# The last attention layer in eight half-batch stages, with softmax sums from ScalarE

## The reference

```python
for e in range(4):                       # quarters of 256 tokens
    xe = x[:, e * n:(e + 1) * n, :]
    xn = _layernorm(xe, norm_w, norm_b)
    m = d // 2 ** e                      # 256, 128, 64, 32 features
    xm = xn[..., :m]
    qs.append(einsum('bnm,dm->bnd', xm, q_w[:, :m]) + q_b)   # ks, vs alike
...                                      # 8 heads of 32, scale d ** -0.5
probs = softmax(q k^T * scale);  attn_out = probs v
out_e = einsum('bnm,om->bno', attn_out[quarter e, :m], o_w[:m, :m]) + o_b[:m]
return concat(pad(out_e) + x_e)          # then _layernorm(x + that)
```

## Time and profile before

| | us |
|---|---|
| median of 3 runs | 2969.61 (2962.3 to 2972.91) |
| profiled execution | 2967.14 |
| its span | 2965.0 |
| PE busy | 2357.0 (79%) |
| DVE busy | 1519.0 (51%) |
| ACT busy | 895.3 (30%) |
| POOL busy | 600.1 (20%) |

### The profile page before, as it was taken

The page is one execution under the profiler, slowest core; times in us unless marked ns, Lnnn a source line. Parts: engine busy times, 40 slices in busy tenths (PEclk is TensorE's granted clock), DMA queues, the critical chain, the costliest instruction groups (busy, mean ns, idle before and its releaser), DMA issues. The chain is left out here.

```text
span 2965.0 us, 44749 instructions
## 1 busy us (share of the span) xinstructions
PE 2357.0 (79%) x18544; PEld 1454.3 (49%) x18544; DVE 1519.0 (51%) x2671; ACT 895.3 (30%) x1265; POOL 600.1 (20%) x340
## 2 busy tenths in 40 slices
PE   3888888999898885856567389898288888898896
PEld 1344544444444443735455245665155555555553
DVE  2445444445454543454645334655566566765662
ACT  0233332333333333423333122221032343333332
POOL 3121111112221101010101033333211122112212
PEclk7899999999999998878888799999588999999998
DMA  6455555444544534566566510110442453245230
GB/s 141 86 101 101 109 103 112 100 94 102 106 108 94 99 60 143 187 199 239 183 232 210 175 59 29 57 57 1 147 118 73 138 145 89 85 138 147 66 91 31
DMA packets 235288, 337.57 MB, mean 114 GB/s; under 512 B 14816, under 2 KB 172880, under 8 KB 234832
## 3 DMA queue, kind: packets, MB, share of 16 engines
q1 hardware_dynamic: 232272, 334.07, 42.4%
q10 hardware_dynamic: 2816, 0.65, 0.1%
HBM read 206.10 MB, written 127.93 MB: 113 GB/s over the span
## 5 line engine op out<-in xcount | busy, mean ns | idle before, releaser
L444 ACT ACTIVATE l0a_probs<-l0a_slot 128x1024 f32<-128x1024 f32 (+1 forms) x256 | 247.4, 970 | 419.5 <-PE l0a_slot L606 419.3
L1620 ACT ACTIVATE l1f_probs<-l1f_slot 128x1024 f32<-128x1024 f32 x240 | 241.0, 1022 | 428.1 <-PE l1f_slot L1793 293.3
L501 DVE TENSOR_REDUCE l0a_rowmax<-l0a_slot 128x4 f32<-128x1024 f32 (+1 forms) x256 | 293.4, 1156 | 126.6 <-PE l0a_slot L606 123.7
L1683 DVE TENSOR_REDUCE l1f_rowmax<-l1f_slot 128x1 f32<-128x1024 f32 x240 | 287.7, 1219 | 100.5 <-PE l1f_slot L1779 100.3
L601 PE MATMUL l0a_slot<-l0a_maskT,l0a_ident 128*128 128x512 bf16 (+1 forms) x512 | 161.6, 400 | 73.7 <-issue 67.9
L1793 PE MATMUL l1f_slot<-l1f_Qs,l1f_Ks 128*128 128x256 f32 x960 | 185.5, 320 | 40.8 <-DVE l1f_rowmax L1683 16.6
L1793 PEld LDWEIGHTS l1f_slot<-l1f_Qs,l1f_Ks 128*128 128x128 f32 x960 | 142.7, 202 | 110.9 <-DVE l1f_rowmax L1683 29.9
L1779 PE MATMUL l1f_slot<-l1f_Ks,l1f_Qs 96*128 96x512 f32 x480 | 172.4, 453 | 29.3 <-DMA l1f_Qs<-kq_rows 16.5
L601 PE MATMUL l0a_slot<-l0a_mask,l0a_ident 128*128 128x512 bf16 (+1 forms) x512 | 150.3, 376 | 25.7 <-issue 23.4
L404 POOL TENSOR_TENSOR l0a_turned<-l0a_turned 128x512 f32<-128x512 f32 x32 | 40.7, 1273 | 634.8 <-DVE l0a_turned L487 634.8
L1738 PE MATMUL l1f_os<-l1f_probs,l1f_V 128*32 128x256 f32 x1920 | 165.6, 397 | 2.0 <-ACT l1f_probs L1620 1.1
(11 more groups left out here) (186 smaller groups left out, 4018.7 us busy)
## 6 DMA issues: line engine op xcount, KB each, us to landing
expert_outputs<-l0f_inter SPq DMA_DIRECT2D x64, 512.0 KB, 2.6
l0f_wide<-expert_outputs SPq DMA_DIRECT2D x32, 1024.0 KB, 9.6
l0a_Qs<-qk_rows SPq DMA_DIRECT2D x96, 256.0 KB, 7.9
l0a_Ks<-qk_rows SPq DMA_DIRECT2D x96, 256.0 KB, 15.0
l1f_Ks<-kq_rows SPq DMA_DIRECT2D x48, 512.0 KB, 6.9
l0f_f<-in_dram SPq DMA_DIRECT2D x10, 2048.0 KB, 15.4
qk_rows<-l0a_hi SPq DMA_DIRECT2D x32, 512.0 KB, 2.8
qk_rows<-l0a_lo SPq DMA_DIRECT2D x32, 512.0 KB, 4.2
```

The source lines that it names most:

```text
L444: exp_ready.by(act.activation(probs[:, t % 2, HG * g:HG * g + HG, 0:reach, :], s[:, :, 0:reach, :], ACT.Exp, scale=SCALE))
L501: max_ready.by(dve.reduce_max(rowmax[:, t, :, 2 * g:2 * g + 2], s[:, :, :, first:2 * P], AX))
L1620: exp_done.by(act.activation(probs[:, half, u - FIRST[i], :], s[:, :], ACT.Exp, scale=SCALE))
L1683: max_done.by(dve.reduce_max(rowmax[:, 2 * u + t:2 * u + t + 1], s[:, :], AX))
```

## The change

In the fourth layer:

1. The hand-written list is replaced by eight equal stages, two a batch, of tr tiles of half a batch, four pv of the half before, and the nat tiles of three stages later; the class `Schedule` walks it, and offsets say which sequence a step belongs to (-1 to 2). K and Q are bounced in one stage and stacked in the next.
2. The sums of the softmax come from the nat tiles. After the maximum, ACT takes the exponential of the nat tile in place, with the negated maximum as bias, and adds along the keys. The tile's last reader is now ACT.
3. The pv step has no matmul of ones. The 8 or 6 sums of a batch are inverted by DVE as 128x8 values and spread over 32 columns a unit; PE transposes that (step `R`, two matmuls with the identity), ACT copies it to SBUF, and DVE multiplies.
4. Wq and its bias are scaled once, so the exponentials take no scale; the sign of the maxima row changes.
5. Placing the maxima (the small DMA on ACT's queue) is a step of its own, in the stage after the transpose.
6. In all layers POOL clears the layer's semaphores at its end.

```diff
+    front = {0: [(1, "xT", 0), (1, "xT", 1), (1, "xT", 2)],
+             1: [(2, "load", 0), (1, "k", 0), (1, "q", 0)],
+             2: [(1, "stack k", 0), (1, "stack q", 0), (-1, "out", 0), (-1, "out", 1)],
+             3: [(1, "k", 1), (1, "q", 1), (-1, "finish", 0)],
+             4: [(1, "stack k", 1), (1, "stack q", 1), (1, "rest of q", 0), (1, "v", 0)],
+             5: [(0, "again", 0), (1, "v", 1), (2, "statistics", 0)],
+             6: [],
+             7: [(2, "normalise", 0)]}
+    for s in range(NSTAGE):
+        i, half = divmod(s, 2)
+        n = len(BATCHES[i])
+        tr = [(0, "tr", 2 * FIRST[i] + n * half + u) for u in range(n)]
+        o, was = divmod(s - 1, NSTAGE)
+        pv = [(o, "pv", HKT * was + j) for j in range(HKT)]
+        o, part = divmod(s + 3, NSTAGE)
+        units = range(FIRST[part // 2], FIRST[part // 2] + len(BATCHES[part // 2]))[2 * (part % 2):2 * (part % 2) + 2]
+        nat = [(o, "nat", 2 * u + t) for u in units for t in range(2)]
+        row = merged(nat[:len(nat) // 2], tr[:2]) + pv[:2] + merged(nat[len(nat) // 2:], tr[2:]) + pv[2:]
+        row = merged(row, front[s])
+        if s % 2 == 0:
+            row += [(0, "R", i - 1) if s else (-1, "R", NB - 1), (o, "mT", part // 2)]
+            placing = o, part // 2
+        else:
+            row[4:4] = [(placing[0], "place", placing[1])]
+            row[6:6] = [(placing[0], "recip", placing[1])]
+        steps += row
...
+            return {"nat": (sum_done, i + 1), "tr": (exp_done, i + 1), "mT": (maxT_ready, i + 1), "out": (summed, (1, NE)[i % 2]),
...
+                if kind == "nat":
+
+                    s = schedule.slot(step)
+                    max_done.wait(act, X, i + 1)
+                    sum_done.by(act.activation(s[:, :], s[:, :], ACT.Exp, bias=negmax[:, i:i + 1].bitcast(f32),
+                                               accum_out=sums[:, i:i + 1]))
...
-                    exp_done.by(act.activation(probs[:, half, u - FIRST[i], :], s[:, :], ACT.Exp, scale=SCALE))
+                    exp_done.by(act.activation(probs[:, half, u - FIRST[b], :], s[:, :], ACT.Exp))
+                if kind == "R":
+                    rows = DH * len(BATCHES[i])
+                    spread_done.wait(act, X, i + 1)
+                    ao_ready.wait(act, X - (i < 2), (3, NB + 1, 1, 2)[i])
+                    spread_ready.by(act.copy(spread[0:rows, i % 2, :], OS[i % 2][0:rows, 1, :]))
...
-                    max_done.by(dve.reduce_max(rowmax[:, 2 * u + t:2 * u + t + 1], s[:, :], AX))
+                    s = arrived(dve, X, step)
+                    max_done.by(dve.reduce_max(negmax[:, i:i + 1], s[:, :], AX, negate=True))
...
+                if kind == "recip":
+                    units = len(BATCHES[i])
+                    cols = slice(2 * FIRST[i], 2 * FIRST[i] + 2 * units)
+                    sum_done.wait(dve, X, cols.stop)
...
-                    for what in range(2):
-                        for u in range(n):
-                            h = BATCHES[i][u][0]
-                            lhsT = ones[:, :] if what else V[:, parity, kt, DH * h:DH * h + DH]
+                    for u in range(units):
+                        h = BATCHES[b][u][0]
+                        last = mm(OS[b % 2][DH * u:DH * u + DH, 0, :], V[:, parity, kt, DH * h:DH * h + DH],
+                                  probs[:, half, u, QW * j:QW * j + QW], start=kt == 0, stop=kt == NT - 1,
```

More of the change, by code:

```diff
@@ L25, in ps, with clear @@
         return ctx.enter_context(nc.psum_tensor(f"{layer}_{name}", shape, dtype))
+    sems = []
+    def clear():
+        nums = sorted(s.num for s in sems)
+        for n in nums:
+            if n - 1 not in nums:
+                nc.gpsimd.sem_clear(range(n, next(m for m in itertools.count(n) if m not in nums)))
+    ctx.callback(clear)
     def sem(name):
-        return ctx.enter_context(nc.semaphore(f"{layer}_{name}"))
+        sems.append(ctx.enter_context(nc.semaphore(f"{layer}_{name}")))
+        return sems[-1]
     return sb, ps, sem
@@ L1336, in tr @@
[L1336 to L1366, removed]
@@ L1377, in nested_width_attention_layer @@
+    slotted = ("xT", "k", "q", "v", "nat", "mT", "tr", "out")
     with ExitStack() as ctx:
@@ L1400, in nested_width_attention_layer @@
         own_ln = LayerNorm(sb, sem, "own", setup, 1)
-        slots = [ps(f"slot{i}", [P, 1024]) for i in range(NSLOT)]
+        schedule = Schedule(steps, slotted, [ps(f"slot{i}", [P, 1024]) for i in range(3)], NSEQ)
+        arrived = schedule.arrived
         OS = [ps(f"os{i}", [P, 2, QW]) for i in range(2)]
@@ L1420, in nested_width_attention_layer @@
+        inverted = signal("inverted", NB); recip_ready = signal("recip_ready", NB); spread_done = signal("spread_done", NB)
+        spread_ready = signal("spread_ready", NB); ao_ready = signal("ao_ready", NB + 1)
         summed = signal("summed", NE)
[L1422 to L1428, removed]
@@ L1460, in loop, with reader @@
[L1460 to L1475 removed]
+        def reader(name):
+            kind, i = name
+            return {"nat": (sum_done, i + 1), "tr": (exp_done, i + 1), "mT": (maxT_ready, i + 1), "out": (summed, (1, NE)[i % 2]),
+                    "xT": (xT_ready[i % 3], None), "v": (v_ready, i + 1), "k": (lo_ready, 2 * i + 1), "q": (lo_ready, 2 * i + 2)}[kind]
@@ L1806, in piece @@
                             col += w
-                (lead_filled if is_ahead else filled).by(last)
-            loop(pe, piece)
+                schedule.put(step, last)
+            schedule.loop(pe, piece)
 def four_layers(nc, x, wq, wk, bq, bk, wv, bv, wo, bo, cos, sin, mask, maskT, ident, ident16,
```

448 lines of the change are left out of this document (204 added, 244 removed).

## The result

The kernel after takes 3077.1 us (median of 4 runs, 3071.96 to 3084.18), the kernel before 2968.02 beside it: ratio 1.0366, 95% interval 1.033 to 1.0402. Slower, as forecast, but by 109 us and not by 33, and outside the range (3053). Its profiled execution has a span of 3078.1 us.

A forecast was written before the change was run, and what follows sets the result against it. Bound: waits on the ring of three PSUM tiles, held by the natural exponential. Full-clock period 102.7 us, 107 with clock; 2251 + 7p gives 3000 us. Range 2925 to 3053 us, to hold eight tenths.

The forecast's parts named there:

- The sign: Whole kernel: slower, 3000 us, 33 over the profiled time; chances slower 0.60, same 0.14, faster 0.26.
- What is removed and added on each engine: Fourth layer, per sequence: PE loses 14.7 us and gains 1.8, to about 70; ACT comes to 69, DVE to 59.
- The pieces of the slot's life: Natural tile's PSUM slot: 0.67 to maximum, 1.29 maximum and hand-over, 1.11 exponential, 0.13 read-out, 0.06 to PE; 3.3 us at least.
- each half stage pays for the exponential: Half stage (two nat, two tr, two pv): chain through the natural exponential takes 4.75 us, against 3.2 of PE.
- the bounces bring the start forward: Fourth layer's start: both bounces first and Q stacked behind K give the first tr near 2158, 15 us earlier.
- The walk through the 75 tiles: One period's tiles written out by slot three back, queue order and engine work: 102.7 us at full clock.
- The clock: PE's granted clock in the steady part taken as 0.94, raising the period from 102.7 to 107 us.
- rival (c): Clock falls to the second layer's level, about 0.85: period 114, 3049 us; chance 0.18 for (c) and beyond.
- the tail: Last exponential's end to the span's end: 32 us, from 34 before.
- (a): Rival: full clock, period 101.4 to 103.9, 2970 us, no change; chance 0.14.
- (b): Rival: exponential in place is cheap, no read-out cost; period 98.2, 2938 us, faster; chance 0.26.
- (d): Rival: sum read-out at its upper bound, 2 us more per period, 3014 us; within the forecast's range, no chance of its own.

The follow-up runs named there:

- e12: Kernel after without the natural tiles' exponentials (sums left at one), with store behind stacks and second load of x behind the reciprocal root: 2857.0 us, period 86.6.
- e3: Kernel after with SP's store moved behind the second pair of stacks, second load of x behind the next statistics' reciprocal root: 3060.4 us, ratio 1.032.
- e15: Kernel after with four zero-weight filler matmuls in PE's waits, store behind the stacks and second load of x behind the reciprocal root: 3033.8 us, period 106.9.
- e8: Kernel before with SP issuing both bounces first, then K's and Q's stacks, at its projections: 2954.0 us, ratio 0.9945.
- e14: Kernel after with four zero-weight filler matmuls ahead of every second transposed tile of a stage: 3077.7 us, ratio 1.0361, period 114.5.
- e1: Kernel after without its 30 exponentials of natural tiles per sequence, sums left at one, tile free at its maximum: 2926.7 us, ratio 0.9858.
- e13: Kernel after with natural exponentials replaced by ones of an SBUF constant, slot free at maximum, transposed tile's exponential first on ACT: 2945.2 us, ratio 0.9916.
- e10: Kernel after with seven filler matmuls on constants ahead of every second transposed tile, output not the reference's: 3141.8 us, ratio 1.0604.

## Why the prediction came out short

**Right.** The sign. What is removed and added on each engine, 69 and 59 us on ACT and DVE. The pieces of the slot's life. That each half stage pays for the exponential: 4.75 against 3.2 us, times 15, is 23 us a sequence; e12 against e3 gives 24.7, with the clock's change in it, and e12 against e15, both near full clock, 20.3. That PE's idle time ends mostly with the natural exponential. That the bounces bring the start forward: 13 us in the kernel before (e8).

**The walk through the 75 tiles.** The transposes of the maxima end every second stage. Their rows in the kernel after, then in e15:

```profile
2582.60 0.27 PE L1756 MATMUL l1f_slot<-l1f_ident,l1f_negmax 128*6 128x128 f32 x1
2605.81 0.27 PE L1756 MATMUL l1f_slot<-l1f_ident,l1f_negmax 128*8 128x128 f32 x1
2635.94 0.27 PE L1756 MATMUL l1f_slot<-l1f_ident,l1f_negmax 128*8 128x128 f32 x1
2671.38 0.27 PE L1756 MATMUL l1f_slot<-l1f_ident,l1f_negmax 128*8 128x128 f32 x1
2698.64 0.27 PE L1756 MATMUL l1f_slot<-l1f_ident,l1f_negmax 128*6 128x128 f32 x1
```

```profile
2569.87 0.27 PE L1773 MATMUL l1f_slot<-l1f_ident,l1f_negmax 128*6 128x128 f32 x1
2591.83 0.27 PE L1773 MATMUL l1f_slot<-l1f_ident,l1f_negmax 128*8 128x128 f32 x1
2615.84 0.27 PE L1773 MATMUL l1f_slot<-l1f_ident,l1f_negmax 128*8 128x128 f32 x1
2648.35 0.27 PE L1773 MATMUL l1f_slot<-l1f_ident,l1f_negmax 128*8 128x128 f32 x1
2675.72 0.27 PE L1773 MATMUL l1f_slot<-l1f_ident,l1f_negmax 128*6 128x128 f32 x1
```

| stages | walk | e15 | after |
|---|---|---|---|
| 5 and 6 | 22.4 | 22.0 | 23.2 |
| 7 and 0 | 24.2 | 24.0 | 30.1 |
| 1 and 2 | 30.7 | 32.5 | 35.4 |
| 3 and 4 | 25.4 | 27.4 | 27.3 |
| period | 102.7 | 105.9 | 116.0 |

Without the chain and at full clock the walk holds to 3 us in this period, 4.2 against the mean of five. Short are the stages with projections and outputs, 1 to 4. Which of their terms was too small is not shown. About 1 us a period is a slip: the terms of the half stage as listed add up to 4.81, not 4.75. And part may be the filler itself: at 2642.92 in e15 four filler matmuls go ahead of a transposed tile whose slot had its last reader done at 2643.22, and the tile goes at 2644.46. So 4.2 is the most that the walk itself was short.

**The step that failed.** "Waits only on the slot three back, queue order and the engine's own work": I walked PE, ACT and DVE, and not SP and POOL. `again` and `finish` were given no time, although their queues now held the root of the next statistics. Stages 7 and 0 show it: by the same rows they take 24.6, 25.8, 26.8, 30.1, 31.1 and 28.1 us in six periods of the kernel after, and 23.8 to 24.7 in those of e3, where the walk had 24.2. This is 4.0 us a period by e3 (115.3 to 111.3), and 7.6 at nearly full clock (114.5 in e14 to 106.9 in e15).

**The clock.** Its value was wrong, 0.94 against 0.82 to 0.85, so rival (c) had the clock. Its price was right by accident: from e3 to e15 the clock gives 4.4 us a period; I had charged 4.3, for much less loss. (The 4.4 are net of what the filler costs.) Half speed is dear only where PE is on the chain. Rival (c)'s price of 11 for 0.85 was too high, though its period of 114 is near. The Trainium skill, page "TensorE: Matmul & The Clock Gate", section "A second HAM failure mode: psum-queue depth-cycling", was right that short idles between PSUM groups cost clock: filled with matmuls, the same order runs at 1.00. Here the lost clock was worth nothing until the chain was gone.

**The sum.** 4.2 (walk), 4.0 (chain) and 0.1 (clock) are the 8.3 us from 107 to 115.3. The split depends on the order of the steps: with the clock taken first it gives 0.8 where I had charged 4.3, and the three are 4.2, 7.6 and -3.5. The first transposed tiles of the first and last sequence and the last exponential divide the 80 us between the forecast and the profiled 3080:

```profile
2166.74 1.05 PE L1761 MATMUL l1f_slot<-l1f_Qs,l1f_Ks 128*128 128x256 f32 x4
2966.51 0.71 PE L1761 MATMUL l1f_slot<-l1f_Qs,l1f_Ks 128*128 128x256 f32 x4 [0.27 <-ACT l1f_probs L1576]
3041.80 1.02 ACT L1576 ACTIVATE l1f_probs<-l1f_slot 128x1024 f32<-128x1024 f32 x1 [0.19 <-PE l1f_slot L1761]
```

Seven periods took 799.8 us and not 743, 57 more. The last sequence took 76 up to the end of its last exponential and not 64, and the tail 35 and not 32, 15 more in all; 4.83 us of the tail are PE's wait for POOL's additions, the same chain. The other 9 are the start, 2166.74 and not 2158. There PE waits twice:

```profile
2147.98 2.70 DVE L162 BATCH_NORM_STATS2 l1f_first_stats<-l1f_xn 128x6 f32<-128x256 f32 x8
2154.05 1.22 PE L1752 MATMUL l1f_slot<-l1f_Ks,l1f_Qs 96*128 96x512 f32 x2 [3.47 <-ACT l1f_slot L1560]
2160.63 2.67 DVE L178 TENSOR_SCALAR l1f_xn<-l1f_xn,l1f_first_mv,l1f_first_rstd 128x256 f32<-128x256 f32 x8
2165.72 1.22 PE L1752 MATMUL l1f_slot<-l1f_Ks,l1f_Qs 96*128 96x512 f32 x2 [4.06 <-ACT l1f_slot L1560]
```

The exponential ends both waits but is not their cause: e1, which has none, stands at the same two places for 3.76 and 4.04 us, for DVE's maximum. Ahead of that maximum DVE works on the statistics, then on the normalising of the next sequence. The forecast of the start had no term for either.

**The rivals.** (a) and (b) fall: a nearly full clock alone (0.94 to 0.96) gives 3077.7 (e14), and an exponential in place costs 1.09 us. (d): the read-out is a separate 0.199 us, overlapped to 0.09 in ACT's spacing (1.09 us exponential at 2594.35, the next at 2595.43), less than the 0.13 taken.

## What to carry to other kernels

Work moved to an idle engine is not free when it becomes a link of every stage's chain. Price it by what it holds (a slot, and the queue behind it), and look for the second hold before removing the first. Walk the queues of SP and POOL like the others: a loop store, stacks, reload, additions, next statistics can set the period, and then clock, order and removed work all show no gain until it is gone. Taking one suspect away at a time understates each; here the pairs (e13, e15, e12) told.

## What was not expected of the hardware

An accumulated sum is a second instruction on ACT (199 ns, 240 times), yet taking it away changed the time by 8 us, not clear of the noise. The spreading copy on DVE takes 0.26 to 0.29 us in 24 of its 32 executions. The other eight, 0.44 to 3.56 us, all fall into an operation of POOL on `total`, and none of the 24 does. The longest lasts as long as POOL's doubling:

```profile
2246.40 3.60 POOL L1521 TENSOR_TENSOR l1f_total<-l1f_total 128x2048 f32<-128x2048 f32 x1 [92.98 <-DMA l1f_total<-x]
2246.56 3.56 DVE L1645 COPY l1f_recip<-l1f_inverse 128x192 f32<-128x192 f32 x1
```

Filler matmuls in PE's waits brought the granted clock of a period from between 0.82 and 0.85 to between 0.94 and 0.96 (e14), and to 1.00 (e10, and e15 in two of three periods).
